# The first attention's PE order: the second maxima unit of each step placed behind the chunk weights

## The reference, cut to what matters

```
h = layernorm(x) * (1 + ca) + sa ; h = dynamic_conv(h)            # B=2, S=1024, 128 channels
q, k, v = ...                                                      # 16 heads, 4 key/value heads, HD=64
kc = k.reshape(B, NH, C, 64, HD)                                   # C = 16 chunks of 64 keys
w = softmax(einsum('bhqd,bhckd->bhcqk', q, kc) * scale, axis=-1)   # softmax within each chunk
chunk_out = einsum('bhcqk,bhckd->bhcqd', w, vc)
sum_w = w.sum(-1) ; combined = (chunk_out * sum_w).sum(2)
out = combined / (sum_w.sum(2) + 1e-09) ; out = out @ w_o.T
```

## Time and profile before

| | us |
|---|---|
| median of 3 timed runs | 2433.64 |
| lowest, highest | 2417.99, 2433.91 |
| the profiled execution | 2423.84 |
| its span, first to last instruction | 2422.0 |
| TensorE busy | 2125.3 (88%) |
| VectorE busy | 1441.4 (60%) |
| ScalarE busy | 1001.4 (41%) |
| mean granted TensorE clock | 0.912 |

### The profile page before, as it was taken

The page is one execution under the profiler, slowest core; times in us unless marked ns, Lnnn a source line. Parts: engine busy times, 40 slices in busy tenths (PEclk is TensorE's granted clock), DMA queues, the critical chain, the costliest instruction groups (busy, mean ns, idle before and its releaser), DMA issues.

```text
span 2422.0 us, 31730 instructions
## 1 busy us (share of the span) xinstructions
PE 2125.3 (88%) x10592; PEld 1215.4 (50%) x10592; DVE 1441.4 (60%) x2497; ACT 1001.4 (41%) x1422; POOL 569.1 (23%) x541
## 2 busy tenths in 40 slices
PE   5999999998796999988769999999969879998974
PEld 3444444444583555545534444444437645555554
DVE  5677777774516665652356777778553366566421
ACT  2444444441234656652224344444412245656411
POOL 0000000000000686784210000000000026687731
PEclk6899999999796899998859999999988879999987
DMA  3000000000200000000410000000020000000014
GB/s 120 5 1 5 1 13 1 1 1 11 89 1 9 1 9 6 1 1 27 145 61 5 1 5 1 13 1 1 1 100 1 1 9 5 5 5 1 1 58 125
DMA packets 41076, 51.36 MB, mean 21 GB/s; under 512 B 7985, under 2 KB 36914, under 8 KB 39218
## 3 DMA queue, kind: packets, MB, share of 16 engines
q1 hardware_dynamic: 39890, 47.18, 6.0%
q0 software_dynamic: 1024, 2.10, 0.3%
HBM read 44.03 MB, written 6.82 MB: 21 GB/s over the span
## 4 chain that ended last, share of the span: by engine, by line
PE 67%; DVE 11%; issue 9%; ACT 8%; POOL 3%; DMA 1%; SPq 1%; DVEq 0%; ACTq 0%; POOLq 0%
PE PS L757 9%; PE PS L702 5%; PE PS L717 5%; PE PS L745 4%; PE PS L707 4%; PE PS L685 4%; PE PS L874 4%; PE PS L914 3%; PE PS L934 3%; PE PS L829 3%; PE PS L917 3%; PE PS L1105 2%; DVE mx L1794 2%; POOL Esum L2291 2%; PE PS L612 2%
## 5 line engine op out<-in xcount | busy, mean ns | idle before, releaser
L1794 DVE TENSOR_REDUCE mx<-PS 128x8 f32<-128x512 f32 x512 | 330.4, 685 | 204.1 <-PE PS L685 199.1
L1424 ACT ACTIVATE EE<-PS 128x1024 f32<-128x1024 f32 x256 | 262.1, 1024 | 333.3 <-PE PS L707 332.6
L1825 DVE TENSOR_TENSOR EE<-EE,PS 128x1024 f32<-128x1024 f32 x256 | 310.0, 1212 | 70.3 <-PE PS L745 70.2
L2291 POOL TENSOR_TENSOR Esum<-Esum,EE 128x512 f32<-128x512 f32 (+3 forms) x320 | 336.9, 1082 | 16.1 <-POOL Esum L2291 10.7
L2245 POOL TENSOR_TENSOR U<-xn,norm_aff 128x1024 f32<-128x1024 f32 x2 | 4.7, 2352 | 1193.0 <-DVE QA L2216 1193.0
L1926 DVE TENSOR_REDUCE mrow<-PS 128x1 f32<-128x512 f32 (+3 forms) x384 | 206.4, 552 | 130.8 <-PE PS L877 103.1
L757 PE MATMUL PS<-EE,Vlater 128*64 128x512 f32 x1024 | 275.7, 617 | 0.0
L702 PE MATMUL PS<-QA,KA 128*128 128x512 f32 x512 | 201.3, 475 | 6.1 <-ACT EE L1424 6.1
L1501 ACT ACTIVATE EE<-PS 128x1024 f32<-128x1024 f32 (+2 forms) x192 | 139.5, 738 | 122.0 <-PE PS L917 119.2
L685 PE MATMUL PS<-KA,QA 128*128 128x512 f32 x512 | 180.9, 433 | 8.5 <-DVE KB L1778 3.4
L707 PE MATMUL PS<-QB,KB 80*128 80x512 f32 x512 | 164.9, 404 | 0.0
(11 more groups left out here) (310 smaller groups left out, 3531.7 us busy)
## 6 DMA issues: line engine op xcount, KB each, us to landing
EE<-in_w SPq DMA_DIRECT2D x48, 192.0 KB, 2.7
V<-in_Wg SPq DMA_DIRECT2D x4, 1024.0 KB, 7.5
EE<-in_Wu SPq DMA_DIRECT2D x4, 1024.0 KB, 7.3
EE<-in_Wd SPq DMA_DIRECT2D x4, 1024.0 KB, 9.4
sorted_out<-U SPq DMA_DIRECT2D x12, 256.0 KB, 3.0
wo<-in_wo SPq DMA_DIRECT2D x4, 512.0 KB, 9.2
wq_s<-in_wq SPq DMA_DIRECT2D x16, 128.0 KB, 2.2
U<-in_hidden SPq DMA_DIRECT2D x3, 512.0 KB, 5.8
```

Source lines behind the costliest of these rows:

```text
L1424: act.activation(EE[i % 2][:, t, :], banks(0), ACT.Exp, scale=QSCALE).then_inc(s["p2_exp"], 1)
L1794: dve.tensor_reduce(mx[:, t, half * 8:half * 8 + 8], banks(5 + x % 2, BANK).rearrange("p (c k) -> p c k", c=8), AX, ALU.max).then_inc(s["p ...
L1825: dve.tensor_tensor(EE[i % 2][:, t, :], EE[i % 2][:, t, :], banks(bank), ALU.mult).then_inc(p3_mul, 1)
L2291: ins = pool.tensor_tensor(Esum[:, h, lo:hi], Esum[:, h, lo:hi], e_tile(t)[:, h, lo - t * P:hi - t * P], ALU.add)
```

## The change

In each step of `head0` on the tensor engine the second unit is issued behind `chunk_weights` instead of behind the first unit; at t = 7 `turn_maxima` is issued behind `chunk_weights` too. No instruction is added, removed or resized, and no semaphore or wait value is different. VectorE, ScalarE, GpSimd and SyncE keep their orders.

```
                     for t in range(NT):
                         scores(i, t)
                         if i + 1 < HEADS:
-                            maxima(i + 1, UNITS0[t])
-                        if t == NT - 1 and i + 1 < HEADS:
-                            turn_maxima(i + 1)
+                            maxima(i + 1, UNITS0[t][:1])
                         if t >= 3 and i >= 1:
                             chunk_weights(i - 1, t - 3)
                         if t < 3 and i >= 2:
                             chunk_weights(i - 2, t + 5)
+                        if i + 1 < HEADS:
+                            maxima(i + 1, UNITS0[t][1:])
+                        if t == NT - 1 and i + 1 < HEADS:
+                            turn_maxima(i + 1)
                         if t >= 4 and i >= 1:
```

## The result

The changed kernel takes 2466.83 us, the median of 4 runs (2462.14 to 2472.1), against 2433.77 for the kernel before (4 runs, 2417.99 to 2438.97). The ratio is 1.0164, with a 95% interval of 1.0115 to 1.0213: slower by 1.6%. The forecast was 2464, with a range of 2441 to 2484.

What follows compares the result with a forecast made beforehand. TensorE's own sequence was taken to bound the heads. Terms 38.0 + 3.2 - 4.7 + 1.3 = 37.8 us gave 2461.6 on the profiled execution, 2471 on the median; 2464 was named, range 2441 to 2484.

Steps and rivals of the forecast that it cites:

- (a): Ordinary steps on TensorE: four changes of array use instead of three, 0.20 us in each of 190 steps, 38.0 us.
- (d): Steps 0 and 1: second unit falls behind the wait for `weigh`, losing 0.45 not 0.40; 26 heads x 0.05, 1.3 us.
- (b): Step t = 7 in non-"q" heads: transposes and chunk weights swap, one more change of use, 16 x 0.20, 3.2 us.
- (c): Step t = 7 in "q" heads 2 to 12: earlier chunk weights bring chunk sums 0.39 earlier, 12 heads, -4.7 us.
- Half price: Rival on array-use changes: only the leave is paid, entering load hidden; 206 steps x 0.10, 2441 us; chance 0.07.
- free: Rival on array-use changes: the lone matmul causes no bubble, only the t = 7 "q" gain remains; 2419 us; chance 0.06.
- VectorE as the bound: Rival: in `low_q` steps, perhaps also steps 2 and 3, VectorE's work exceeds the step; 2471 to 2482 us; chance 0.13.
- Faster: Rival: early chunk weights free VectorE so both TensorE waits, before lines 717 and 745, vanish; 2392.6 us; chance 0.02.

Runs made afterwards that it cites:

- Experiment 1's first kernel: Kernel before with only the second unit moved behind the chunk weights, transposes of t = 7 left in place; 2472.13 us against 2431.69, ratio 1.0176.
- Experiment 3: Chunk weights computed over the whole array (128 weight rows, output wrong), in the kernel before and in the changed kernel; ratios to the kernel before 1.0063 and 1.0085.
- experiment 4: Kernel before with the second unit behind the values, ahead of the next scores, and VectorE's `weigh` ahead of the second reduction; 2421.77 us against 2430.96, ratio 0.9972.
- experiment 6: Changed kernel with 16 weight columns instead of 128 in the second unit, same 512 columns streamed, output wrong; 2463.1 us in one execution.
- experiment 3's second kernel: Changed kernel with chunk weights over the whole array (128 weight rows, output wrong); ratio to the kernel before 1.0085.
- experiment 5: Kernel before with both units as a pair, and the transposes of t = 7, moved behind the chunk weights; 2496.68 us in one execution.
- experiment 4, `weigh` first: Kernel before with only VectorE's `weigh` put ahead of the second reduction, TensorE's order unchanged; ratio 1.0114.

## Why the prediction was right, point by point

- **(a) The array's use, 0.20 in 190 steps, 38.0 us.** Right in cause and size. Experiment 1's first kernel holds this term with (d): 38.4 us against 38.0 + 1.3. A quiet step is longer by 3.23 - 3.03 = 0.20. The edges at the lone matmul are 0.33, 0.43 and 0.42, forecast as 0.33, 0.43 and 0.44. Experiment 3 removes the edges and keeps the move, and the quiet steps' price is gone; experiment 4 keeps the move and the number of changes, and it is gone too.
- **(b) Plain heads at t = 7, 3.2 us.** Half of that. The last step with what follows is 8.31 against 8.21 (8.62 against 8.50 in "k" heads), 0.10 to 0.12, so about 1.7 us. The term was mis-sized because I gave the transposes the edges of a 128-column matmul. Their weights have 16 columns (the form 128*16 in rows 6), and entering costs with such weights next to nothing, as experiment 6 shows. So do the rows of the changed kernel, head 7:

```profile
313.96 0.63 PE L707 MATMUL PS<-QB,KB 80*128 80x512 f32 x2
314.52 0.49 PE L745 MATMUL PS<-r_parts,spread 64*128 64x512 f32 x2
314.94 1.04 PE L692 MATMUL PS<-consts,mx 128*16 128x128 f32 x8
315.92 1.08 PE L757 MATMUL PS<-EE,Vlater 128*64 128x512 f32 x4
```

  The eight transposes take 0.98 between 64-row and 64-column matmuls, where they took 0.97 behind line 707. What is new is the leave of 0.10 between 707 and 745: 0.56 instead of the 0.47 from 707 to the transposes.
- **(c) q heads at t = 7, -4.7 us.** 9.24 against 9.61, 0.37 instead of 0.39, 12 x 0.37 = 4.4 us. Right. TensorE's wait before line 717 fell to 10.7, forecast about 9.
- **(d) t = 1, 1.3 us.** Steps t = 0 and 1 together are 3.20 + 3.59 = 6.79 against 3.02 + 3.34 = 6.36 in q heads: 0.43, forecast 0.45. Right. It is small only because TensorE is late too: experiment 3's second kernel, without the edges, shows about 0.24 at t = 1 and again at t = 3.
- **The sum**, 37.8, was 35.3 in the heads. The median moved by 33.1 us. That 2464 comes within 3 us of the measured 2466.83 is partly luck: the working gave 2461.6 on the profiled execution and 2471 on the median, and I chose between them. The profiled execution came to 2466.99, because the heads cost 2.5 us less than the sum and the untouched code 7.9 us more, which the sum did not have.
- **Rivals.** Half price and free are excluded by the step of 3.23. VectorE as the bound shows itself otherwise (experiment 5), and not here: with `low_q` the steps t = 4 to 6 are 0.19 to 0.22 longer, as the quiet ones are. The upper end of this rival, 2482, was added up wrongly; 2461.6 + 9 + 10 is 2481, which changes nothing in the range. Faster failed where it was said to: the early chunk weights gain 0.37 a head and no more.

## What to carry to other kernels

Where TensorE is full, count in its order how often the part of the array in use changes (whole, row halves, column halves): here each further change cost about 0.20 us at full clock, although no instruction was added, and only a pitch read between two rows shows it, not a wait. A matmul could be moved far at no price in the quiet steps, where it landed beside its own kind; before moving work on one engine, follow the bank it holds on the other, since `weigh` ahead of the reduction cost 18 us with one order of TensorE and gained 10 with another.

## What the runs showed of the hardware that was not expected

The entering edge depends on the width of the weights: 0.42 for a lone 512-column matmul with 128 weight columns, 0.33 with 16. The 64-column values have smaller edges: eight in one use take 1.87 where two blocks of four take 2.02, 0.15 less. And the parts that no kernel here touched vary by some 20 us between executions. The stretch behind the last head, of some 690 us, is shortest, 687.1 us, where its mean granted clock is highest, 0.89 (experiment 3, second kernel), and longest, 700.7 us, at 0.86 (experiment 4, `weigh` first), while the heads of the two batches of one execution, at clock 1.00, agree within 0.2 us.
